# Four DMA copies of the mixing matrices instead of TensorE copies, and a burst of small products spread over four blocks

## The chip, the core and the metric

The kernel runs on one core of a Trainium2 chip. The metric is the device time of one execution in microseconds (us). The engines that matter here are TensorE (PE in the profile, its weight loads PEld), VectorE (DVE), ScalarE (ACT), GpSimd (POOL) and SyncE (SP). SP, ACT and POOL also issue DMAs; the name of such an issue in the profile is SPq, ACTq or POOLq.

## The reference

The program is two residual layers over x of shape 32 x 32 x 512 (1024 rows of 512 numbers). The first one begins with a small mixing of the 32 channels of each sample, by one of 16 matrices, chosen by a number that comes with the sample:

```python
def _L0_cond_ref(x, weights, condition):      # weights 16 x 32 x 32
    W = weights[condition]
    return jnp.einsum('bct,bcd->bdt', x, W)

x = x + _L0_ffn_ref(_L0_cond_ref(x, L0_cond_weights, itok_B_0_15), ...)
x = x + _L1_ffn_ref(_L1_cond_ref(x, itok_B_8_3872, ...), ...)
```

`_L0_ffn_ref` routes each row to 2 of 16 experts (softmax, best groups, best 2) and adds a shared expert. `_L1_cond_ref` convolves each of the 32 channels along time with a kernel that is computed from a few parameters, for channel h and time l:

```python
Cs = Cc * (jnp.exp(dtA) - 1.0) / A
K = 2.0 * jnp.einsum('hn,hnl->hl', Cs, jnp.exp(P)).real
```

`_L1_ffn_ref` is a dense layer with a latent branch and a layer norm.

## The kernel before

The program is written engine by engine, and the order of the instructions on each engine is the order in which they stand in the code. Engines wait for each other on semaphores (`wait_ge`), whose names are used below.

**The front** works on 8 tiles of 128 rows, 4 samples of 32 channels each. For each tile a block-diagonal matrix `wbd` of 128 x 128 is filled with the four chosen 32 x 32 matrices, so that one TensorE product mixes the tile. The 16 matrices come by one DMA of ACT's queue into `wraw`, on 32 partitions. A block of the diagonal on partitions 32b to 32b+31 has to be copied from the same partitions, so the matrices are needed four times, one below the other. Before, TensorE makes these copies: 8 products with a 32 x 32 identity fill banks 6 and 7 with four copies each (`wall_done`). DVE copies the blocks of seven tiles out of bank 6, ACT those of tile 2 out of bank 7, each block by an instruction whose place comes from a register. The registers are loaded from `condr` beforehand (`picked_matrices`).

TensorE then mixes tile i (`mixr_done`), ACT copies the result to `xstage` (`x_row`) and sends it to DRAM (`xrow`), TensorE transposes it, ACT writes the high part `ah`, and DVE the low part `al`. Every second tile TensorE adds the router's products (`router_logits`), which need `ah` and `al` of two more tiles. ACT waits once, between its first two tiles, for the router's loads (`router_in`), which stand behind `wraw` in its DMA queue. Beside this, DVE makes the low part `swl` of the shared expert's weights (`split_lo`), and after the front it runs the long chain of small steps of the routing. TensorE meanwhile has the shared expert's products (`shared_products`). Inside of one of them, `middle_product`, stand the two products over the chosen experts (`rank_products`), which wait for the routing (`msk_ok`).

**The blocks.** The rows go in 31 blocks of 128 through the experts. Each step n of the loop on TensorE has 8 products of 128 x 128 for block n (`L1606`), the output product of block n-2 (`L1574`) and the 4 transposes of block n+2 (`L1568`). POOL gathers the rows of each block by indirect DMA and scatters the results, and SP loads the experts' weights. An instruction on 32-bit numbers stands in the order once, and has two records in the trace, so that the 8 products are 16 records.

**The time kernel** of the convolution is made in parts along the blocks by DVE, ACT and POOL. Its last part is 32 small products on TensorE (128 x 16 weights, 64 columns), which stand all in step n = 15 behind that step's transposes. ACT copies the result at n = 16 (`kout`), DVE adds to it at n = 17, SP stores it at n = 18, and reads it back spread out for the convolution at n = 23 to 25.

## Time and profile before

| | |
|---|---|
| times of three runs | 343.67 (median), 340.64 and 344.4 us |
| the profiled execution: its own time | 343.47 us |
| its span, first to last instruction | 341.6 us |
| TensorE busy in the span | 324.8 us |
| mean granted clock of TensorE | 0.990 |

The profile is of one execution, and its own time stands 0.2 us from the median of the three runs. The span leaves out 1.9 us of that time. The rows further down are of this execution. Busy times of TensorE are modelled from the starts of its instructions, so that in the timeline the last instruction of a group overlaps the next group; the chain of waits counts each stretch of time once.

### The profile page before, as it was taken

The page shows a single profiled execution, that of the slowest core. Times are in us where ns is not written, and L with a number is a line of the kernel's source. Part 1 is how long each engine was busy: PE and PEld are TensorE (multiplying, and loading weights), DVE is VectorE, ACT ScalarE, POOL GpSimd, SP SyncE. Part 2 cuts the span into 40 slices and gives each one's busy share as a digit, 9 for nine tenths or more (in the row PEclk, how much of TensorE's full clock was granted, in tenths as well). Part 3 has the DMA queues.
Part 4 walks back from the last instruction along what each step waited for, and adds up shares of the span by engine and source line. Part 5 has one row for each costly group of instructions (what it writes and reads, how often), then busy time and mean ns, then how long its engine had stood idle before and what let it go on. Part 6 is the DMA issues. An engine that isn't in the chain of part 4 may idle for free.

```text
span 341.6 us, 5497 instructions
## 1 busy us (share of the span) xinstructions
PE 324.8 (95%) x1945; PEld 245.8 (72%) x1945; DVE 187.4 (55%) x375; ACT 115.3 (34%) x199; POOL 109.8 (32%) x131
## 2 busy tenths in 40 slices
PE   8998899999999599999998899899999999999994
PEld 2566788988887288888686444468888787888872
DVE  3747896888365122365469469537322446442366
ACT  1571312323722123363006833832231424222120
POOL 8243004356577546663400000699200000000000
PEclk9999999999999879999999999999999999999999
DMA  6999920796686629999969986000000000100002
GB/s 194 327 405 405 384 70 13 221 316 205 188 269 219 199 69 328 317 318 378 406 236 412 388 279 216 2 1 0 2 0 0 3 0 31 63 31 0 2 21 101
DMA packets 32830, 59.93 MB, mean 175 GB/s; under 512 B 7213, under 2 KB 8081, under 8 KB 32804
## 3 DMA queue, kind: packets, MB, share of 16 engines
q1 hardware_dynamic: 25764, 48.95, 41.6%
q0 software_dynamic: 4992, 8.42, 7.2%
q10 hardware_dynamic: 2048, 2.21, 1.8%
q8 instruction: 16, 0.26, 0.3%
q14 instruction: 10, 0.08, 0.1%
HBM read 55.02 MB, written 12.40 MB: 197 GB/s over the span
## 4 chain that ended last, share of the span: by engine, by line
PE 80%; DVE 10%; issue 5%; POOL 2%; ACT 2%; DMA 1%; ACTq 0%; DVEq 0%; POOLq 0%
PE bank L1606 15%; PE bank L435 13%; PE bank L437 12%; PE bank L436 12%; PE bank L1574 7%; PE bank L1679 5%; PE bank L1568 4%; PE bank L1434 2%; DVE acc L1259 2%; PE bank L1688 1%; PE bank L1384 1%; PE bank L1466 1%; PE bank L1390 1%; PE bank L1509 1%; DVE osum L1307 1%
## 5 line engine op out<-in xcount | busy, mean ns | idle before, releaser
L1606 PE MATMUL bank<-xt,ew 128*128 128x128 f32 x496 | 62.4, 280 | 0.0
L1606 PEld LDWEIGHTS bank<-xt,ew 128*128 128x128 f32 x496 | 59.6, 196 | 0.8 <-issue 0.7
L639 POOL DMA_INDIRECT xg<-xrow,tokx x31 | 33.3, 1073 | 38.9 <-DVE tokx L1077 25.2
L646 POOL DMA_INDIRECT ytok<-yout,dstx x31 | 31.9, 1029 | 33.3 <-DVE yout L1189 20.3
L1348 DVE TENSOR_TENSOR sq<-rel 128x512 f32<-128x512 f32 x16 | 13.3, 834 | 37.0 <-ACT rel L888 37.0
L1574 PE MATMUL bank<-ew,bhid 128*128 128x512 f32 x62 | 31.7, 595 | 0.0
L792 ACT ACTIVATE xt<-bank 128x512 f32<-128x512 f32 x31 | 18.4, 598 | 31.9 <-PE bank L1568 24.6
L1568 PEld LDWEIGHTS bank<-ident,xg 128*128 128x128 f32 x124 | 15.1, 141 | 16.1 <-issue 14.0
L435 PE MATMUL bank<-ah,uph 128*128 128x512 f32 x64 | 25.2, 394 | 0.9 <-issue 0.9
L435 PE MATMUL bank<-dnh,sqh 128*128 128x512 f32 x64 | 25.2, 393 | 0.4
L436 PE MATMUL bank<-dnl,sqh 128*128 128x512 f32 x64 | 24.9, 390 | 0.0
L437 PE MATMUL bank<-dnh,sql 128*128 128x512 f32 x64 | 24.9, 390 | 0.0
L437 PE MATMUL bank<-ah,upl 128*128 128x512 f32 x64 | 24.9, 389 | 0.0
L436 PE MATMUL bank<-al,uph 128*128 128x512 f32 x64 | 24.9, 389 | 0.0
L686 POOL TENSOR_TENSOR dnl<-dnraw,dnh 128x512 fp32r<-128x512 f32 x8 | 10.5, 1359 | 44.4 <-ACT dnh L855 44.4
L1189 DVE COPY yout<-bank 128x512 f32<-128x512 f32 x31 | 21.4, 689 | 2.6 <-PE bank L1574 0.6
L888 ACT ACTIVATE rel<-bank 128x512 f32<-128x512 f32 x16 | 9.6, 599 | 38.5 <-PE bank L437 38.4
L1200 DVE SCALAR_TENSOR_TENSOR bhid<-bank,b12d,bsil 128x128 f32<-128x128 f32 x15 | 5.3, 351 | 27.4 <-issue 21.3
L1568 PE MATMUL bank<-ident,xg 128*128 128x128 f32 x124 | 18.6, 274 | 0.9 <-issue 0.6
L1679 PE MATMUL bank<-toep,u_t 128*32 128x512 f32 (+3 forms) x256 | 18.7, 435 | 0.7 <-ACT u_t L831 0.7
L1351 DVE TENSOR_TENSOR sql<-sq,sqh 128x512 fp32r<-128x512 f32 x16 | 12.0, 751 | 11.2 <-PE bank L437 6.3
L1200 DVE SCALAR_TENSOR_TENSOR bhid<-bank,b,bsil 128x128 f32<-128x128 f32 x16 | 5.6, 348 | 20.2 <-ACT bsil L804 14.9
(316 smaller groups left out, 619.5 us busy)
## 6 DMA issues: line engine op xcount, KB each, us to landing
ew<-in_L_ffn_ew SPq DMA_DIRECT2D x51, 256.0 KB
ew<-in_L_ffn_ew SPq DMA_DIRECT2D x21, 512.0 KB, 11.9
toep<-kpad SPq DMA_DIRECT2D x4, 1536.0 KB, 17.6
acc<-in_x SPq DMA_DIRECT2D x4, 512.0 KB, 7.2
xrow<-xstage ACTq DMA_DIRECT2D x4, 512.0 KB, 7.7
yg_lo<-ytok SPq DMA_DIRECT2D x4, 512.0 KB, 4.9
yg_hi<-ytok SPq DMA_DIRECT2D x4, 512.0 KB, 8.1
upraw<-in_L_ffn_up_w SPq DMA_DIRECT2D x1, 2048.0 KB, 14.3
```

Of the source, the lines that this page charges most:

```text
L435: pe.matmul(dst, lh, rh, start=(start and k == 0), stop=False)
L436: pe.matmul(dst, lh, rl, start=False, stop=False)
L437: mm = pe.matmul(dst, ll, rh, start=False, stop=(stop and k == n_k - 1))
L639: pool.indirect_dma_start(xg[:, n % XGS, :], None, xrow, bass.IndirectOffsetOnAxis(ap=tokx[:, n:n + 1].bitcast(U32), axis=0), bounds_check ...
L646: pool.indirect_dma_start(ytok, bass.IndirectOffsetOnAxis(ap=dstx[:, n:n + 1].bitcast(U32), axis=0), yout[:, n % YOS, :], None, bounds_che ...
L792: act.activation(xt[:, n % 2, :, :], bank[n % 2][:, :].rearrange("p (k n) -> p k n", k=KC), ACT.Copy)\
L1189: dve.tensor_copy(yout[:, n % YOS, :], bank[6 + n % 2][:, :]).then_inc(yout_ok, 1)
L1348: tt(sq[:, v % 2, :], rel[:, v % 2, :], rel[:, v % 2, :], ALU.mult).then_inc(sq_ok, 1)
L1568: mm = pe.transpose(bank[n % 2][:, k * P:(k + 1) * P], xg[:, n % XGS, k * P:(k + 1) * P], ident[:, :])
L1574: pe.matmul(bank[6 + n % 2][:, :], bhid[:, n % BHS, :], ew[:, ring(n), W3], start=True, stop=True)\
L1606: mm = pe.matmul(bank[2 + n % 2][:, w * P:(w + 1) * P], ew[:, ring(n), col + k * P:col + (k + 1) * P], xt[:, n % 2, k, :], start=(k == 0), ...
L1679: mm = pe.matmul(bank[g % 3][j * B:(j + 1) * B, 0:T - k * P], u_t[:, h0 + j, k, :], toep[:, (h0 + j) % TS, k * P:T], start=(k == 0), stop= ...
```

## The change

The mixing matrices are loaded four times by DMA, each copy onto its own 32 partitions, and in another place in memory. The TensorE copies and their semaphore are gone; DVE and ACT copy the blocks out of `wraw`. SP no longer waits for the TensorE copies ahead of its weight loads. On DVE the comparison `before` moves ahead of the wait for the matrices, and `split_lo(0)` moves from tile 5 to tile 4. In `middle_product` one more group of three products stands ahead of `rank_products`. The 32 small products of the time kernel are spread over the steps n = 14 to 17, eight in each, and the three steps that follow (ACT, DVE, SP) are each two blocks later.

```diff
-        act.dma_start(wraw[:, :, :], cond_w.rearrange("k c d -> c k d")).then_inc(wraw_in, 16)
+        for b in range(BT):
+            act.dma_start(wraw[b * C:(b + 1) * C, :, :], cond_w.rearrange("k c d -> c k d")).then_inc(wraw_in, 16)
...
-        act.wait_ge(wall_done, 2)
+        act.wait_ge(wraw_in, 16 * BT)
         act.wait_ge(wbd_ok, 1)
...
-        dve.wait_ge(wall_done, 1)
-        for i, conds in dve_conds:
-            for b in range(BT):
-                dve.tensor_copy(diagonal(i, b), matrix(6, b, conds[b])).then_inc(wbd_ok, 1)
         dve.wait_ge(const_ok, PLACES)
         link(tt(before[:, :, :], prow[:, 0:E].unsqueeze(1).broadcast_to([P, E, E]),
                 prow[:, 0:E].unsqueeze(2).broadcast_to([P, E, E]), ALU.is_lt))
+        dve.wait_ge(wraw_in, 16 * BT)
+        for i, conds in dve_conds:
+            for b in range(BT):
+                dve.tensor_copy(diagonal(i, b), matrix(b, conds[b])).then_inc(wbd_ok, 1)
...
+            if i == 4:
+                split_lo(0)
             if i == 5:
-                split_lo(0)
...
-        pe.wait_ge(wraw_in, 16)
-        for w in (6, 7):
-            for b in range(BT):
-                mm = pe.matmul(bank[w][b * C:(b + 1) * C, :], ident[0:C, 0:C],
-                               wraw[:, :, :].rearrange("c k d -> c (k d)"), start=True, stop=True)
-            mm.then_inc(wall_done, 1)
...
-            split3(pe, bank[CBANK[1]][:, :], weights, tokens, 1, stop=False)
+            split3(pe, bank[CBANK[1]][:, :], weights, tokens, 2, stop=False)
             rank_products()
...
-            if n == 15:
-                pe.wait_ge(bd_ok, 1)
-                pe.wait_ge(lhs_ok, 2)
-                for m in range(HT // KQ):
-                    for lhs, rhs in ((lre_k, rre_k), (lim_k, rim_k)):
+            if KSTEP <= n < KSTEP + HT // KQ:
+                if n == KSTEP:
+                    pe.wait_ge(bd_ok, 1)
+                    pe.wait_ge(lhs_ok, 2)
+                m = n - KSTEP
+                for lhs, rhs in ((lre_k, rre_k), (lim_k, rim_k)):
```

**ACT at the start of the program**, before: one load of the matrices (`wraw`), then the router's three loads.

```order
L701 DMA wraw<-in_L_cond_weights 32x16x32
L702 DMA rwraw<-in_L_ffn_router_w 128x64
L703 DMA rb<-in_L_ffn_router_b 128x16
L704 DMA rb<-in_L_ffn_router_bias 128x16
L723 ACT_TABLE_LOAD
L723 ACTIVATE std<-warm 128x1
L442 TENSOR_LOAD condr
```

And with the change, where `wbd` is now filled out of `wraw`:

```order
L701 DMA wraw<-in_L_cond_weights 32x16x32 x4
L702 DMA rwraw<-in_L_ffn_router_w 128x64
L703 DMA rb<-in_L_ffn_router_b 128x16
L704 DMA rb<-in_L_ffn_router_bias 128x16
L723 ACT_TABLE_LOAD
L723 ACTIVATE std<-warm 128x1
L442 TENSOR_LOAD condr
```

Three DMAs of the matrices have come ahead of the router's loads, and the block copies wait for all four.

**TensorE at step 15 of the block loop**, before. `rre_k`, `rim_k`, `lre_k` and `lim_k` are the operands of the time kernel's products, `xt` and `ew` those of the block's.

```order
L1574 MATMUL bank<-ew,bhid 128x512
L1568 MATMUL bank<-ident,xg 128x128 x4
L1630 MATMUL bank<-rre_k,lre_k 16x64 x4
L1630 MATMUL bank<-rim_k,lim_k 16x64 x4
L1630 MATMUL bank<-rre_k,lre_k 16x64 x4
L1630 MATMUL bank<-rim_k,lim_k 16x64 x4
L1630 MATMUL bank<-rre_k,lre_k 16x64 x4
L1630 MATMUL bank<-rim_k,lim_k 16x64 x4
L1630 MATMUL bank<-rre_k,lre_k 16x64 x4
L1630 MATMUL bank<-rim_k,lim_k 16x64 x4
L1606 MATMUL bank<-xt,ew 128x128 x8
```

With the change, from the transposes of step 14 on (line numbers are 5 lower):

```order
L1563 MATMUL bank<-ident,xg 128x128 x4
L1625 MATMUL bank<-rre_k,lre_k 16x64 x4
L1625 MATMUL bank<-rim_k,lim_k 16x64 x4
L1601 MATMUL bank<-xt,ew 128x128 x8
L1569 MATMUL bank<-ew,bhid 128x512
L1563 MATMUL bank<-ident,xg 128x128 x4
L1625 MATMUL bank<-rre_k,lre_k 16x64 x4
L1625 MATMUL bank<-rim_k,lim_k 16x64 x4
L1601 MATMUL bank<-xt,ew 128x128 x8
L1569 MATMUL bank<-ew,bhid 128x512
L1563 MATMUL bank<-ident,xg 128x128 x4
```

The row of 32 small products is cut into four rows of 8, with 13 instructions of a block between two of them.

**DVE in the front**, before, from its comparison to the end of the low parts. `al` are the low parts of the 8 tiles, `swl` those of the shared expert's weights.

```order
L933 TENSOR_TENSOR before<-prow 128x256
L936 TENSOR_TENSOR rwc<-rwraw,rwc 128x4x16
L944 TENSOR_TENSOR al<-bank,ah 128x4x128 x6
L940 TENSOR_TENSOR swl<-swraw,swh 128x1024
L949 CAST dimh<-sw 128x16
L950 RECIPROCAL sw<-sw 128x16
L944 TENSOR_TENSOR al<-bank,ah 128x4x128 x2
L940 TENSOR_TENSOR swl<-swraw,swh 128x1024
```

With the change (the comparison stands ahead of the block copies now):

```order
L936 TENSOR_TENSOR rwc<-rwraw,rwc 128x4x16
L944 TENSOR_TENSOR al<-bank,ah 128x4x128 x5
L940 TENSOR_TENSOR swl<-swraw,swh 128x1024
L944 TENSOR_TENSOR al<-bank,ah 128x4x128
L950 CAST dimh<-sw 128x16
L951 RECIPROCAL sw<-sw 128x16
L944 TENSOR_TENSOR al<-bank,ah 128x4x128 x2
L940 TENSOR_TENSOR swl<-swraw,swh 128x1024
```

The first `swl` has moved one `al` up, and `dimh` with the reciprocal stays behind the sixth `al`.

## Rows read from the trace of the kernel before

**Rows 1.** Waits of PE, whole run (waiting line, releaser: total us, times, longest).
```profile
PE bank L1630 <- issue: 3.7, 5, 1.1
...
PE bank L1475 <- DVE w2t L991: 0.9, 1, 0.9
...
PE bank L1416 <- DVE al L944: 0.8, 1, 0.8
```

**Rows 2.** Timeline of PE, 0 to 30 us (start, us, engine, line, tiles, shape, records).
```profile
1.51 3.78 PE L1384 MATMUL bank<-warm 128*128 128x512 f32 x4 [1.51 <-DVE warm L920]
5.23 3.64 PE L1390 MATMUL bank<-wraw,ident 32*32 32x512 f32 x16
8.79 3.78 PE L1434 MATMUL bank<-acc,wbd 128*128 128x512 f32 x4
...
14.93 1.02 PE L1434 MATMUL bank<-acc,wbd 128*128 128x512 f32 x2
```

**Rows 3.** Timeline of ACT, 0 to 42 us; ACTq is its issue of a DMA.
```profile
0.80 0.40 ACTq L701 DMA_DIRECT2D wraw<-in_L_cond_weights  x1
...
2.24 0.45 ACTq L704 DMA_DIRECT2D rb<-in_L_ffn_router_bias  x1
...
11.40 0.25 ACT L734 ACTIVATE rwc<-rwraw 128x64 fp32r<-128x64 f32 x1
```

**Rows 4.** DVE: loads of condition numbers (view of tile condr), and its timeline.
```profile
L442 DVEq TENSOR_LOAD <-condr x7: 336/343/593, 3.2 to 5.6; - x7
...
7.34 6.08 DVE L931 COPY wbd<-bank 32x32 f32 x28 [4.22 <-PE bank L1390]
```

**Rows 5.** DMA issues at 0 to 1.3 and 2.4 to 3 us: KB, us to landing.
```profile
acc<-in_x SPq DMA_DIRECT2D x1, 512.0 KB, 4.0
wraw<-in_L_cond_weights ACTq DMA_DIRECT2D x1, 64.0 KB, 1.9
...
rb<-in_L_ffn_router_bias ACTq DMA_DIRECT2D x1, 8.0 KB, 7.5
```

**Rows 6.** DMA queues, 0 to 12 us: packets, MB, share (q1 SP's, q10 ACT's).
```profile
q1 hardware_dynamic: 1557, 2.76, 72.8%
q10 hardware_dynamic: 960, 0.11, 6.2%
```

**Rows 7.** DMA queues, 20.5 to 22.5 us.
```profile
q10 hardware_dynamic: 206, 0.42, 53.6%
q1 hardware_dynamic: 207, 0.40, 51.5%
```

**Rows 8.** Chain that ended last, 0 to 80 us (start us, us, what).
```profile
40.18 0.23 PE bank L435
```

**Rows 9.** Chain that ended last, 108 to 130 us.
```profile
113.13 0.33 PE bank L1630 x10
...
114.93 0.50 issue
...
118.27 1.49 PE bank L1630 x46
119.76 3.67 PE bank L1606 x16
...
124.73 1.79 PE bank L1606 x16
```

**Rows 10.** Windows at 108 to 128 us: length, busy by engine, granted clock, DMA share, GB/s.
```profile
113.00:116.00 3.00, 1.17 (x16) 0.44 (x14) 0.00 (x0) 0.19 (x1) 2.12 (x3) 1.00 0.90 251
116.00:117.00 1.00, 0.15 (x4) 0.23 (x4) 0.00 (x0) 0.00 (x0) 0.96 (x1) 0.71 0.88 326
...
119.00:123.00 4.00, 4.00 (x44) 3.80 (x34) 0.69 (x2) 0.20 (x1) 2.04 (x2) 0.50 0.03 4
```

**Rows 11.** Timelines of SP and of ACT, 96 to 122 us.
```profile
112.55 1.42 SPq L527 DMA_DIRECT2D ew<-in_L_ffn_ew  x2
...
118.34 0.37 ACT L804 ACTIVATE bsil<-bank,b 128x128 f32<-128x128 f32 x1 [5.15 <-remote]
```

33 lines of the change are left out of this document (16 added, 17 removed).

## The prediction

> **What bounds the kernel now.** TensorE is busy for 324.8 of the 341.6 us, so I read its waits first. Over the whole run the longest in sum is at line 1630, the 32 small products of the time kernel: 3.7 us in five pieces, put down to "issue", which means that no semaphore in the trace explains them. Behind it come 0.9 us for the routing at line 1475 and 0.8 us for the low parts at line 1416 [rows 1]. Next I read the chain of waits at these places. The chain is TensorE's own for nearly all of the run, so a microsecond that TensorE loses or gains in the front or in the block loop is one of the total.
>
> In the front the timeline of TensorE shows two warm-up products to 5.29 us, the copies of the matrices to 8.87, and the first mixing product at 8.79 [rows 2]. The copies are the gate: DVE starts its 28 block copies at 7.34, after 4.2 us of waiting for them [rows 4], while the first load of x, issued before 1.3 us, took 4.0 us and so was in by 5.3 us [rows 5]. In the block loop the chain has the small products from 113.1 to 119.8 us, then a block's 16 records that take 3.67 us where the same 16 take 1.79 us a block later [rows 9].
>
> **The small products.** Their work is short: 46 of the 64 records take 1.49 us [rows 9], 32 ns each, so all 64 take 2.1 us. They have 119.76 - 113.13 = 6.63 us, so 4.5 us are stall. And the stall has a sequel. TensorE had 1.17 us of busy time between 113 and 116 us; the granted clock was 0.71 in the next microsecond, and 0.50 from 119 to 123 [rows 10]. That is the lower of the two levels, 1.2 GHz, and the following block pays 3.67 - 1.79 = 1.9 us for it [rows 9]. The places together lose 4.5 + 1.9 = 6.4 us. The page "TensorE: Matmul & The Clock Gate" of the Trainium skill (Part 1) says that an idle spell brings the clock to half rate until sustained work releases it; the trace agrees, with 0.50.
>
> With the change eight products follow the transposes of each of steps 14 to 17. Their work stays on the path, a fourth of 2.1 us each time, since TensorE has no idle time there to hide it. What of the stall stays depends on its cause, which the trace does not tell. For the burst as the cause speaks that the program has only one such burst (128 product and load records in a row) and only one such stall, and that the last 46 records then run freely. Against it speaks that others stall too: SP needs 1.42 us for two issues at 112.55, and ACT starts a step at 118.34 after 5.15 us of waiting for something that the profile calls "remote" [rows 11]. I take it that the burst is the cause and that cutting it frees the 6.4 us. The other end is 0. The steps moved behind it (ACT, DVE, SP, two blocks later each) cost nothing: their instructions are the same, and the store of the result at step 20 has three blocks before it is read back at step 23. If that cover failed, the read-back would be late, and its first user is the convolution, behind all blocks.
>
> **The matrices by DMA.** Removed are TensorE's copies, 3.64 us. TensorE would still have to wait for DVE's first four block copies, a seventh of 6.08 us, 0.87 us [rows 4]. So the first mixing product comes 0.87 us after the last copy of the matrices has landed, or after DVE is free, whichever is later. DVE's seven loads of condition numbers start until 5.6 us and take 0.34 each [rows 4], and the comparison stands behind them now: it is free at about 6.4 us. If the DMAs were in by then, mixing would begin at 7.3 instead of 8.8, a gain of 1.5 us.
>
> Are they? One copy alone took 1.9 us from its issue at 0.80 [rows 3, 5]. The next three are issued every 0.42 us, the last at 2.1. But by then the loads of x are on the same DMA engines, issued from before 1.3 us on. Three things bear on the last copy's landing.
> - If ACT's queue were on its own, it would land at 2.1 + 1.9 = 4.0 us. This is the lower end.
> - The nearest row in place and queue is the load of the router's bias: issued by ACT at 2.24 us, 8 KB, landed after 7.5 us, at 9.7 [rows 3, 5]. A copy of the matrices issued at 2.1 has eight times its bytes, in rows of 128 bytes.
> - The queues share in turns. Where both had work, ACT's moved 206 packets in two microseconds and SP's 207 [rows 7]. One matrix copy is 32 x 16 = 512 packets (rows of 128 bytes), so three are 1536. Before, SP's queue needed the whole of 0 to 12 us for its 1557 packets [rows 6]. With one packet of ACT for one of SP, the last copy lands at about 12 us or shortly after, say 13.5 with its own packets' time and the landing on top. This is the upper end, somewhat stretched.
>
> I take 12.0, nearest to the count of packets, since both queues have work from 2 us on. Mixing then begins at 12.0 + 0.87 = 12.9 instead of 8.8: a loss of 4.1 us (range: gain of 1.5 to loss of 5.6). Nothing hides it, because everything up to the routing hangs on the mixing. That TensorE now idles from 5.3 us on costs nothing further by these rows: the first mixing passes run slowly as it is, 3.78 us for four records against 1.02 for two later on [rows 2].
>
> A rule of the skill speaks against this part. "DMA: Bandwidth & Descriptors", section Issuing engines are not separate DMA queues, says that DMAs from all engines run on the same 16 DMA engines and interleave, whoever issued them. The trace agrees by its 206 to 207. By the rule the sum is the one that follows; without it, with a landing at 4.0 us, it would be 5.6 us lower.
>
> Behind the copies in ACT's queue stand the router's three loads. ACT needed them at 11.40 us before, without waiting [rows 3], 4.1 us after the block copies began. With the new order they are the last in the queue, and might come somewhat more than 4.1 us after the matrices. I count 0.4 us (0 to 1.5). SP's dropped wait gives nothing: at that place in its queue the copies had long been made.
>
> **The two orders.** `split_lo(0)` one tile earlier uses idle time of DVE ahead of the sixth tile. It can give at most the 0.8 us that TensorE waits at line 1416 [rows 1]; ACT's `ah` of the last tile is late next, so I count 0.4. In `middle_product` three products of 0.23 us [rows 8], 0.7 us, move ahead of the wait of 0.9 us for the routing [rows 1]. They fit into it whole, 0.2 us of wait remain, and the routing gets its products no later: 0.7 us.
>
> **Sum.** 343.47 - 6.4 (small products) + 4.1 (matrices late) + 0.4 (router's loads) - 0.4 - 0.7 = 340.5 us. The profiled execution stands 0.2 us below the median of the three runs, so this is also about 0.9% below the median.
>
> **Rivals.**
> - **The stall is not the burst's.** ACT and SP were slow in the same stretch [rows 11], so a congestion of the DMAs or of memory may hold everyone until about 118 us, whatever TensorE has to do. The split then gives nothing, and the late matrices decide: 340.5 + 6.4 = 346.9 us, slower than before. It is slower from the point where less than 3.4 us of the 6.4 come back. Chance 0.28.
> - **The stall is partly left.** Eight products at a time still stutter, but TensorE does not idle long enough to lose its clock, or the reverse: about half, 3.2 us, comes back. 343.7 us, no change. Chance 0.20.
> - **The matrices are early.** The copies interleave better than one for one, or the descriptors reach the engines ahead of those of x; mixing begins at 7.3 us. Against it stands the router's bias with its 7.5 us. With the stall gone: 340.5 - 4.1 - 1.5 - 0.4 = 334.5 us. Chance 0.14; with a landing between, at 8 us, it would be 336.5.
> - **The forecast**, stall gone and matrices late, has 0.38.
>
> **How the numbers follow.** One per cent, 3.4 us, is about what this measurement can tell from no change. Within the forecast the landing's bounds alone give 337 to 342, within the second rival 344 to 348.4. The range 335.5 to 348.5 leaves out the ends of the early and of the late case. Faster by over 1% (below 340.2) are most of the early case, 0.12, and a good half of the forecast, 0.21, where the landing is before 11.7 us: 0.33. Slower by over 1% (above 347.1) are near half of the first rival and a bit of surprise: 0.19. The rest, 0.48, is within 1%.
>
> **What would show it.** In the changed profile: the landing of the four `wraw` loads, and the first mixing product 0.9 us after the last (I expect 12.9; 7.3 if the early rival holds). The four groups of small products should take 0.5 us each, with no wait "issue" and a granted clock of 1.00 between 100 and 125 us; under the first rival the same gaps appear at other instructions of TensorE. The wait at line 1475's successor should be about 0.2 us. The prediction is wrong if the front's end moves by less than 1 us, or if a stall of some microseconds stands in the block loop at all.

## The result, and where the time went

The changed kernel takes 349.4 us in the median of four runs (349.0 to 350.5), against 342.7 us for the kernel before beside it (four runs, 340.6 to 344.4): a ratio of 1.021, with a 95% interval of 1.016 to 1.026. The forecast was 340.5. In this and in every ratio below, a run more than 1.5% above the fastest of its kernel is left out. The profiled execution after has 349.01 us, a span of 347.2 us against 341.6.

**First view: the whole run.** The page's row of busy time, and part 4, the chain that ended last, of the changed kernel:

```profile
PE 320.9 (92%) x1929; PEld 243.1 (70%) x1929; DVE 187.1 (54%) x375; ACT 114.7 (33%) x199; POOL 110.9 (32%) x131
...
PE 63%; DVE 11%; DMA 9%; issue 8%; POOL 3%; SPq 1%; ACT 1%; another core or an unknown queue 1%; ACTq 1%; DVEq 0%; POOLq 0%
```

TensorE works 3.9 us less (324.8 before) in a span 5.6 us longer. The chain has 63% of the span on TensorE, where it had 80% before, and 9% on DMAs, where it had 1%.

**Second view: by stage.** The block loop has one group of 16 product records a block, so the start of the first one marks where a kernel stands. The small products of step n stand ahead of block n+1. These columns are worked out from such groups of each profile: start of block 0, then the length from block 0 to 13, 13 to 17, 17 to 24, 24 to 30, and from there to the end of the span. All kernels of the study but e4 stand here, since the experiments are read from it too.

```
kernel                  block 0   0-13   13-17   17-24   24-30  30-end   span
before                    62.85  39.41   22.30   21.59   18.93  176.52  341.6
after                     65.09  39.41   20.11   22.64   22.68  177.27  347.2
e1_orders                 61.62  39.41   22.62   21.59   18.93  176.54  340.7
e2_four_loads             66.50  39.41   22.21   21.59   18.93  177.26  345.9
e3_four_parts             59.86  39.41   22.88   22.23   21.94  178.07  344.4
e5_late_sw3               64.91  39.41   22.82   22.23   18.93  177.00  345.3
e6_sbuf_copies            66.31  39.41   20.07   21.59   18.93  176.60  342.9
e7_no_products            60.07  39.41   22.53   21.59   18.93  176.58  339.1
e8_no_chain               62.81  39.41   22.33   21.59   18.93  176.53  341.6
e9_chain_on_dve           62.58  39.41   19.26   21.59   18.93  178.04  339.8
e10_warm_after            63.30  39.41   21.66   22.23   22.64  177.56  346.8
e11_loads_early           59.70  39.41   21.75   21.59   18.93  177.12  338.5
e12_orders_chain_dve      58.83  39.41   18.90   21.59   18.93  176.54  334.2
e13_short_gathers         59.66  39.41   23.06   21.59   18.93  176.55  339.2
e14_gathers_held          62.51  39.41   17.33   27.68   19.83  178.65  345.4
e15_matrices_first        59.52  39.41   23.01   22.23   22.33  177.51  344.0
e16_best_first            61.27  39.84   16.62   21.59   18.93  176.45  334.7
e17_best_capped           62.01  39.41   16.39   23.12   21.60  177.87  340.4
e18_change_mended         59.39  39.41   17.40   22.23   21.00  177.27  336.7
```

From before to after: front +2.24, blocks 13 to 17 -2.19, 17 to 24 +1.05, 24 to 30 +3.75, the rest +0.75, together 5.6 us. The front and the stretch of the stall, on which the prediction spent its words, cancel. What made the kernel slower lies between blocks 17 and 30, mostly in the last six.

**The front.** Answering to [rows 2] and [rows 4], the timelines of TensorE and of DVE in the changed kernel (start, length, line, what, and in brackets the wait before it), and the DMAs of the matrices:

```profile
1.51 3.78 PE L1385 MATMUL bank<-warm 128*128 128x512 f32 x4 [1.51 <-DVE warm L920]
11.80 3.75 PE L1429 MATMUL bank<-acc,wbd 128*128 128x512 f32 x4 [6.50 <-DVE wbd L934]
```

```profile
6.04 0.42 DVE L929 TENSOR_TENSOR before<-prow 128x256 f32<-128x256 f32 x1 [2.93 <-issue]
10.91 6.49 DVE L934 COPY wbd<-wraw 32x32 f32 x28 [4.45 <-DMA wraw<-in_L_cond_weights]
```

```profile
L701 ACTq DMA_DIRECT2D wraw<-in_L_cond_weights x4: 399/508/512, 0.8 to 2.3; - x4
...
DMA to landing us min/median/max: 1.9/5.4/8.4
```

The fourth copy is issued at 2.30 us and takes 8.4: it lands at 10.7, DVE starts at 10.9, the mixing at 11.8, 3.0 us later than before and 1.1 after the landing. By block 0 the delay is down to 2.2 us, so 0.8 came back, which fits the two orders.

**The stall.** The chain of waits of the changed kernel from block 15 on, and three windows (the last columns are the granted clock, the share of the DMA engines and GB/s), to set beside [rows 9] and [rows 10]:

```profile
112.43 0.35 PE bank L1625 x16
112.78 1.76 PE bank L1601 x14
114.54 0.39 issue
...
115.32 1.04 issue
...
117.04 0.74 issue
...
119.85 0.78 issue
```

```profile
113.00:116.00 3.00, 1.93 (x16) 1.64 (x15) 0.46 (x1) 0.60 (x1) 2.39 (x3) 1.00 0.76 253
116.00:119.00 3.00, 1.70 (x4) 0.65 (x4) 0.00 (x0) 0.00 (x0) 2.39 (x3) 1.00 0.87 248
119.00:123.00 4.00, 3.03 (x35) 2.67 (x36) 0.95 (x2) 0.85 (x2) 0.15 (x1) 1.00 0.40 118
```

A fourth of the small products takes 0.35 us. But the waits "issue" are still there, now mostly at the lines of the block's own products (1601, 1569, 1563): from 111 us on they add up to 4.0 us, against 4.3 before. Only the clock held: 1.00 where it had been 0.50 before.

**The last blocks.** ACT's timeline near its step 23, and from the chain of waits the pieces that lead to it:

```profile
150.64 0.60 ACT L792 ACTIVATE xt<-bank 128x512 f32<-128x512 f32 x1 [2.52 <-PE bank L1563]
154.00 1.06 ACT L823 ACTIVATE sw3h<-sw3raw 128x1024 fp32r<-128x1024 f32 x1 [2.76 <-DMA kpad<-kout]
154.97 0.35 ACT L804 ACTIVATE bsil<-bank,b12d 128x128 f32<-128x128 f32 x1
```

```profile
148.30 5.68 DMA kpad<-kout
...
158.62 7.26 DMA xg<-xrow,tokx
```

ACT stands 2.8 us at its step 23, waiting for the store of the time kernel's rows, which SP now issues from 146.8 us on and which lands at 154.0, 7.2 us later. Behind ACT stand the blocks, and when they go on, a gather needs 7.3 us. Before, the same store was issued at 139.7, and no engine waited for it:

```profile
139.67 2.01 SPq L539 DMA_DIRECT2D kpad<-kout  x4
146.85 1.05 ACT L823 ACTIVATE sw3h<-sw3raw 128x1024 fp32r<-128x1024 f32 x1
```

ACT came to its step 23 there 7.2 us after the store's first issue, so there was hardly any time to spare: in three kernels that store at step 18, as before (e4, e6 and e7), ACT waited 0.5 to 1.0 us for it.

### The profile page after: what moved, and what is told of

Same layout as the page of the kernel before. It is cut to its first block, busy times and chain, and to the rows that moved or that the text cites. A ratio compares the mean times of both kernels' runs of the same rounds, so it can differ in the third digit from the quotient of the medians.

```text
span 347.2 us, 5467 instructions
## 1 busy us (share of the span) xinstructions
PE 320.9 (92%) x1929; PEld 243.1 (70%) x1929; DVE 187.1 (54%) x375; ACT 114.7 (33%) x199; POOL 110.9 (32%) x131
## 4 chain that ended last, share of the span: by engine, by line
PE 63%; DVE 11%; DMA 9%; issue 8%; POOL 3%; SPq 1%; ACT 1%; another core or an unknown queue 1%; ACTq 1%; DVEq 0%; POOLq 0%
PE bank L435 12%; PE bank L436 11%; PE bank L437 11%; PE bank L1601 9%; PE bank L1569 4%; DMA xg<-xrow,tokx 3%; PE bank L1429 3%; PE bank L1563 3%; PE bank L1674 3%; DMA wraw<-in_L_cond_weights 2%; DVE acc L1260 2%; DMA kpad<-kout 2%; DVE upl L1280 1%; DMA ytok<-yout,dstx 1%
## 5 line engine op out<-in xcount | busy, mean ns | idle before, releaser
L1601 PE MATMUL bank<-xt,ew 128*128 128x128 f32 x496 | 61.3, 276 | 2.8 <-issue 1.6
L1601 PEld LDWEIGHTS bank<-xt,ew 128*128 128x128 f32 x496 | 58.1, 192 | 4.3 <-issue 2.3
L685 POOL TENSOR_TENSOR dnl<-dnraw,dnh 128x512 fp32r<-128x512 f32 x8 | 10.5, 1349 | 45.3 <-ACT dnh L855 45.3
L1429 PE MATMUL bank<-acc,wbd 128*128 128x512 f32 x16 | 10.6, 765 | 6.5 <-DVE wbd L934 6.5
## 6 DMA issues: line engine op xcount, KB each, us to landing
ew<-in_L_ffn_ew SPq DMA_DIRECT2D x21, 512.0 KB, 11.9
toep<-kpad SPq DMA_DIRECT2D x4, 1536.0 KB, 17.6
```

The source lines that it names most:

```text
L1429: pe.matmul(bank[2 * (i % 3) + 1][:, :], wbd[:, i, :], acc[:, i, :], start=True, stop=True)\
L1601: mm = pe.matmul(bank[2 + n % 2][:, w * P:(w + 1) * P], ew[:, ring(n), col + k * P:col + (k + 1) * P], xt[:, n % 2, k, :], start=(k == 0), ...
```

## The experiments

Ratios are to the kernel before, run on the same chip beside each, with 95% intervals. A stage's length is from the table above.

### The parts of the change, each alone

e1_orders is the two changes of order:

```diff
-            if i == 5:
-                split_lo(0)
+            if i == 4:
+                split_lo(0)
...
-            split3(pe, bank[CBANK[1]][:, :], weights, tokens, 1, stop=False)
+            split3(pe, bank[CBANK[1]][:, :], weights, tokens, 2, stop=False)
```

> The kernel before with the two changes of order alone (the split of the low parts one tile earlier, two products ahead of the routing in place of one). Theory, from the changed kernel's trace: its first block of experts starts 2.24 us later while its first mixing product starts 3.0 us later, so the orders give 0.75 us; the first block should start at 62.1 instead of 62.85 and the time be 0.8 us below the kernel before. Rival: the wait for the routing grows by what is taken away, because the routing itself is late: no change, 62.8.

Measured: 340.4 us, ratio 0.998 (0.994 to 1.003), and in the profile block 0 starts 1.23 us earlier. The waits are 0.5 at line 1417 (0.8 before) and 0.2 for the routing (0.9 before):

```profile
PE bank L1417 <- DVE al L944: 0.5, 1, 0.5
PE bank L1476 <- DVE w2t L992: 0.2, 1, 0.2
```

That is near the prediction's 0.4 + 0.7. A gain of this size is below what the timing tells.

e2_four_loads is the matrices by DMA alone (the diff of the change without its other parts).

> The kernel before with the matrices loaded in four copies by DMA, nothing else. Theory: only the start of the mixing moves, 3.0 us later (11.8 instead of 8.8), and all behind it, so the time is 3 us above the kernel before and the block loop's own intervals stay as they were. Rival: the loads of x take the place of the copies and the later mixing finds its tiles ready, so that half of it comes back by the first block: +1.5 us.

Measured: 1.016 (1.009 to 1.023). The first mixing product starts at 12.58, block 0 at 66.50, 3.65 us later, and the block loop is untouched up to block 30. Next to nothing of the delay (3.79 us at the mixing) comes back, and the part behind the blocks is 0.74 us longer.

e3_four_parts is the products in four parts and the three later steps alone.

> The kernel before with the small products in four parts and the three steps behind them two blocks later, nothing else. Theory A: ACT waits at step 23 for the stored kernel rows, which are stored two blocks later and land only after that step; in the changed kernel this cost 3.7 us from block 24 to block 29, and the parts themselves gained 1.1 us up to block 18. So +2.6 us, with ACT's wait for the store in the trace and blocks 25 to 29 late. Theory B: the late loss of the changed kernel came from its front being shifted against the transfers, not from the store: -1 to -2 us, and blocks 24 to 30 every 3.1 us.

Measured: 1.017 (1.010 to 1.024), or 5.8 us (5.0 between the medians), twice what theory A gave. The late loss is there, 3.0 us from block 24 to 30, with ACT waiting 5.1 us for the store; 1.6 us more are lost behind the blocks, which was not explained. But blocks 13 to 17 take 22.88 us against 22.30: alone, the split doesn't shorten the stall at all. And this profile showed something in the front, which it has in common with the kernel before:

```profile
5.22 1.99 PE L1390 MATMUL bank<-wraw,ident 32*32 32x512 f32 x16
7.44 2.00 PE L1434 MATMUL bank<-acc,wbd 128*128 128x512 f32 x4 [0.23 <-DVE wbd L931]
9.28 0.64 PE L1398 MATMUL bank<-ident,xstage 128*128 128x128 f32 x4
```

The same copies took 3.64 us and the same four mixing records 3.78 in the profile before [rows 2]. The clock came up some microseconds earlier in this execution, and block 0 starts at 59.86 instead of 62.85. The view of windows doesn't show this, since it prints 1.00 where the trace has no record of the clock: the trace's first record, at the level 1.00, stands at 5.4 us here and at 14.0 in the profile before. Of the twelve profiles of kernels in which TensorE makes the copies, five have it at 4.9 to 6.0 us and seven at 13.3 to 14.1. The times of the kernel before fall in two groups as well: of thirteen in one call, six took 339.6 to 341.5 us and seven 343.0 to 344.0. That these are the same two kinds is likely, and not shown run by run.

e4_two_parts cuts the products in two, at steps 14 and 15, and leaves the later steps where they were.

```diff
-            if n == 15:
+            if 14 <= n < 14 + HT // KQ // 2:
...
-                for m in range(HT // KQ):
+                for m in range((n - 14) * 2, (n - 14) * 2 + 2):
```

> The kernel before with the small products in two parts of 16 at steps 14 and 15, and the copy, the sum and the store where they were (steps 16, 17, 18). Theory A (the store's lateness is what costs): no late loss, and the gain of the parts alone, -1 to -2 us; the spell in which TensorE loses time without a semaphore stays, at other instructions, while GpSimd issues its gathers and scatters back to back. Rival, the burst of 64 short instructions is itself the cause: half of the stall, -3 us or better. Under a third, any split loses: +0.5 us or more.

Measured: 0.999 (0.995 to 1.003), no gain, by six of its eleven runs (340.7 to 342.4 us). The other five took 347.2 to 349.7 us, the profiled one among them, so its stages aren't in the table. What set them apart was not looked into.

### Is it the store that makes the last blocks late?

```diff
-            if n == 23:
+            if n == 26:
                 act.wait_ge(kpad_in, 16 * KQ)
...
-            elif n == 24:
+            elif n == 27:
                 dve.wait_ge(swh_ok, 3)
```

> The changed kernel whole, and ACT's step 23 (the wait for the stored kernel rows and the copy of a shared expert's weights into their place) made step 26, DVE's step 24 behind it made 27. Theory A: ACT's wait for the store is what made blocks 25 to 30 late; now the store has landed before ACT comes to it, blocks 24 to 30 start every 3.1 us, and the time is 3 to 4 us below the changed kernel, 1.0 to 1.2% above the kernel before. Rival: the delay in this stretch is in the transfers (the late loads of weights, the store, and the reads of the matrix rows one on the other, with gathers of 7 us), ACT only showed it: 0 to 1 us below the changed kernel, 2% above the kernel before.

Measured: 1.014 (1.009 to 1.019) against 1.021 for the change, and blocks 24 to 30 take 18.93 us, to the hundredth what they took before. ACT's timeline has the copy without a wait:

```profile
158.83 0.60 ACT L792 ACTIVATE xt<-bank 128x512 f32<-128x512 f32 x1 [0.93 <-PE bank L1563]
159.32 1.05 ACT L823 ACTIVATE sw3h<-sw3raw 128x1024 fp32r<-128x1024 f32 x1
```

So the 3.75 us of these blocks are the price of ACT's wait and of what followed from it. The timing gives 2.6 of them; blocks 13 to 17 take 22.82 us in this profile, so the change's 20.11 did not come back.

### What is the stall?

e7_no_products:

```diff
-                for m in range(HT // KQ):
+                for m in range(1):
```

> The kernel before with 28 of the 32 small product pairs' halves left out: of the four parts only the first m is computed, 8 products in place of 32, so that the time kernel is wrong in most of its rows; all waits and later steps are as before. Burst theory: with no burst there is no stall: the time is 6.4 + 1.6 (the work left out) = 8 us below the kernel before, and TensorE has no gap of its own between 105 and 120 us. Theory of GpSimd's catch-up (its gathers and scatters run back to back from 102.5 to 117 us, and all gaps of TensorE in six profiles lie in that stretch): the gaps stay and move to the blocks' own instructions, and only 1.6 to 3.5 us come back.

Measured: 0.999 (0.993 to 1.005). TensorE's timeline with a quarter of the products:

```profile
110.11 0.30 PE L1630 MATMUL bank<-rre_k,lre_k 128*16 128x64 f32 x8
111.38 0.27 PE L1630 MATMUL bank<-rim_k,lim_k 128*16 128x64 f32 x2 [0.97 <-issue]
112.85 0.22 PE L1630 MATMUL bank<-rim_k,lim_k 128*16 128x64 f32 x1 [1.19 <-issue]
...
115.69 0.37 PE L1630 MATMUL bank<-rim_k,lim_k 128*16 128x64 f32 x2 [1.13 <-issue]
115.99 3.78 PE L1606 MATMUL bank<-xt,ew 128*128 128x128 f32 x16
```

Sixteen records take 5.9 us, and the block behind them 3.78, twice its length. Three quarters of the work gone, and blocks 13 to 17 take 22.53 us (22.30 before). The burst is not the cause: TensorE is drawn out there with a fourth of the work as well.

e8_no_chain and e9_chain_on_dve ask whether it is GpSimd being late. GpSimd runs 15 small operations of the time kernel between two gathers, and has to catch up afterwards. The diff is that of e9; e8 has two copies on GpSimd in the place of the 15 operations.

```diff
-        move(0, 15)
-        pool.wait_ge(s4v_ok, POWERS)
-        link(pool.tensor_scalar(w[NR], er, -1.0, None, ALU.add))
...
-        pool.tensor_tensor(w[CIN], w[X1], w[X2], ALU.subtract).then_inc(s4p_ok, 1)
-        move(15, NB + AHEAD)
+        move(0, NB + AHEAD)
...
+        def s4_coef():
+            link(dve.tensor_scalar(w[NR], er, -1.0, None, ALU.add))
...
+            elif n == 11:
+                s4_coef()
```

> The kernel before without GpSimd's chain of 15 small operations between its gathers (two copies stand in their place, so the coefficients of the time kernel are wrong); everything else is as before. Theory of the catch-up: without the 5 us of the chain GpSimd isn't late, its gathers and scatters don't run back to back afterwards, and TensorE has no gaps and no lower clock between 105 and 125 us: 5 to 8 us below the kernel before. Burst theory: the stall stays at the small products, and at most 0.6 us comes back.

> The kernel before with the same chain of 15 operations run by DVE at its step 11, which is empty, in place of GpSimd; the same numbers are computed. Theory of the catch-up: as without the chain, less what DVE's chain costs if it holds a block (15 operations and their waits, 2 to 3 us against some 1.5 us of free time a block): 4 to 7 us below the kernel before. Burst theory: no change, or up to 1.5 us slower for the held block.

Measured: without the chain 1.002 (0.996 to 1.007), and the stall as before, 22.33 us. With the chain on DVE 0.990 (0.982 to 0.998), and the stretch 3.0 us shorter (3.4 in e12, which has the same edit), while the part behind the blocks is 1.5 us longer. The four runs are 335.6, 339.9, 340.0 and 341.6 us, and the ratio leaves out the last, which is the profiled one; with it the medians give 0.995. So the shorter stretch is the firm result here, and the gain in time rests on e12. The two contradict the plain catch-up theory: taking the chain out altogether should help at least as much. The profile of e8 shows GpSimd issuing back to back all the same, from 93.2 to 107.4 (with one rest of 1.0 us) and from 110.6 to 118.3 us.

e11_loads_early takes the weights' loads out of the stretch:

```diff
-        return d * 7 // 5 if d < RING else LATE_STEPS[d - RING]
+        return d if d < RING else LATE_STEPS[d - RING]
```

> The kernel before with the loads of the later experts' weights issued as soon as a place is free (one at each of the steps 0 to 13) in place of seven in five steps each; the last three stay at steps 20 to 22. So between 105 and 120 us only gathers and scatters use the DMA engines. Theory (the weights' loads together with the gathers hold up the engines' instructions there): no gaps of TensorE between 105 and 120 us, 5 to 7 us below the kernel before. Rival (the loads have no part in it): the gaps stay, ending 16 us after the start of block 13, and the time is the same within 1 us.

Measured: 0.994 (0.988 to 1.000), blocks 13 to 17 21.75 us. The ratio leaves out three of the eight runs (342.7 to 343.6 us), which look like the later kind of e3's two; against the kernel before's earlier kind (340.6 in the mean) four of the other five are level, at 340.3 to 340.8. The gaps stay, so the loads have little part in it.

By now fourteen profiles showed one thing in common. GpSimd issues its gathers and scatters back to back, one each 1.33 us, and TensorE's last gap ends 0.9 to 1.5 us after the end of that stretch in all but one (e11, 2.8). In the profile before this is the last issue of the stretch, and the last gap ends at 118.27 [rows 9]:

```profile
115.94 1.03 POOL L639 DMA_INDIRECT xg<-xrow,tokx x1 [0.31 <-issue]
```

Two experiments ask which of the two follows the other:

```diff
+            rows = 16 if 15 <= n <= 20 else P
...
-            pool.indirect_dma_start(xg[:, n % XGS, :], None, xrow,
+            pool.indirect_dma_start(xg[0:rows, n % XGS, :], None, xrow,
```

```diff
             wait(pool, bx_done, n - XGS + 1)
+            if 17 <= n <= 20:
+                pool.wait_ge(bh_done, n - 2)
```

> The kernel before with the gathers 15 to 20, which GpSimd issues back to back from 102.5 to 117 us, fetching 16 rows each in place of 128, so that six blocks work on rows of earlier ones and the result is wrong there. Theory C1 (the packets of the gathers, with the weights' loads, congest the stretch and hold up all engines): no gaps of TensorE between 105 and 120 us, or less than half, 3 us or more below the kernel before. Theory C2 (it is GpSimd's issuing itself, whatever it moves): if a short gather takes GpSimd as long, the gaps stay and end 1.0 to 1.5 us after GpSimd's last issue; no change. Theory C3 (neither): the gaps stay and their end no longer follows GpSimd's.

> The kernel before with one more wait on GpSimd: gathers 17 to 20 each wait for the products of the block three before theirs, so that GpSimd can't run ahead while TensorE stands. In 13 of 14 profiles TensorE's last gap ended 0.9 to 1.5 us after GpSimd's back-to-back stretch. If GpSimd's stretch is what holds the others (C1 or C2), it is now cut at about 113 us, and TensorE's last gap ends at 113 to 115 instead of 118.3, with blocks 16 to 19 late by their gathers (3 to 4 us from issue to landing against 3 us of lead), 0 to 3 us below the kernel before. If the order is the other way (GpSimd stops because TensorE stood and no more rows are due), the gaps still end at about 118 us and the kernel is 1 to 4 us slower.

Measured: with short gathers 1.003 (0.998 to 1.007), and 23.06 us from block 13 to 17. A gather of 16 rows occupies GpSimd for 0.92 to 0.94 us (the first 1.00), one of 128 rows for 1.03 (the first 1.10), so its stretch is nearly as long as before, and so is the stall: the gathers' packets don't matter. The scatters and the loads of weights were left as they were.

```profile
112.67 0.92 POOL L640 DMA_INDIRECT xg<-xrow,tokx x1 [0.30 <-issue]
```

With the gathers held 1.011 (1.004 to 1.017; two timed runs) in all, but the stretch falls to 17.33 us. GpSimd's timeline in that kernel:

```profile
109.25 1.03 POOL L641 DMA_INDIRECT xg<-xrow,tokx x1 [1.54 <-PE bank L1608]
110.59 1.01 POOL L648 DMA_INDIRECT ytok<-yout,dstx x1 [0.30 <-issue]
112.92 1.02 POOL L641 DMA_INDIRECT xg<-xrow,tokx x1 [1.32 <-PE bank L1608]
114.25 1.01 POOL L648 DMA_INDIRECT ytok<-yout,dstx x1 [0.30 <-issue]
118.94 1.03 POOL L641 DMA_INDIRECT xg<-xrow,tokx x1 [3.67 <-PE bank L1608]
```

It rests where it ran on before. TensorE passes 40 of the 64 small records within 0.8 us from 113.2 us on, has gaps of 0.41 and 0.45 us during and right behind the scatter of 114.25, and is through at 116.1. What this kernel loses in all, it loses behind the stretch: 27.68 us from block 17 to 24, with late gathers, and 2.1 us behind the blocks.

### The landing of the matrices, and TensorE's clock

e6_sbuf_copies loads the matrices once, as before, and makes the other three copies from that one inside the local memory, 96 packets of 2048 bytes in place of 1536 of 128:

```diff
+        act.wait_ge(wraw_in, 16)
+        for b in range(1, BT):
+            act.dma_start(wraw[b * C:(b + 1) * C, :, :], wraw[0:C, :, :]).then_inc(wraw_in, 16)
```

> The kernel before with one load of the matrices from memory, as before, and the three other copies made from it by DMA within the local memory, in rows of 2048 bytes (96 packets in place of 1536), issued by ACT behind the router's loads; TensorE makes no copies. Theory (the late landing is a matter of the packets that stand in turn with those of x): the copies are issued at about 5 us and land at 7 to 8.5, the first mixing product starts at 8 to 9.5, about where it was before: the time is 0 to 1 us from the kernel before, 3 to 4 below the four loads. Rival (anything behind the loads of x waits for them, whatever its count): landing at 10 or later, and 2 us or more above the kernel before.

Measured: 1.015 (1.009 to 1.021). ACT's timeline:

```profile
2.85 2.35 ACTq L705 DMA_DIRECT2D wraw<-wraw  x3
12.04 0.98 ACT L731 ACTIVATE wbd<-wraw 32x32 f32 x4 [5.31 <-DMA wraw<-wraw]
```

A sixteenth of the packets, with the same bytes, are in at 11.9 us, later than the 10.7 of the change. The three copies were issued from 2.85 us on, their first packet moved at 8.5, and they landed at 10.4, 11.0 and 11.9, while the last load of x, issued at 2.69, landed at 12.6. So it isn't packets in turn with those of x. In the change the same is seen: the second, third and fourth load of the matrices landed at 5.8, 8.0 and 10.7 us, and the loads of x issued just ahead of them at 5.5, 7.3 and (the third and the fourth) 9.0 and 10.5. A copy issued behind the loads of x comes in with them, whatever the number of its packets.

e10_warm_after is the change with WARM = 5 in place of 2.

> The changed kernel whole, with five warm-up products on TensorE in place of two, which fill its idle time from 5.3 us on; the matrices arrive as late as before. Theory: the idle time has a price of its own, since TensorE meets the mixing at the lower clock; with the filling the first four mixing records take 2.0 us, as in the one profile where the clock was up early, and not 3.75, and the first block starts 1.7 to 2 us earlier (63.2 instead of 65.1). The prediction's step, by which the idling costs nothing further, says: no change.

Measured, by the profile (two timed runs, 1.016): block 0 at 63.30 instead of 65.09, though its matrices were 0.6 us later.

```profile
1.52 7.51 PE L1385 MATMUL bank<-warm 128*128 128x512 f32 x10 [1.52 <-DVE warm L920]
12.40 1.95 PE L1429 MATMUL bank<-acc,wbd 128*128 128x512 f32 x4 [3.37 <-issue]
```

1.95 us instead of 3.75 for the same four records, half: the two levels of the clock. This is one profile, and by e3 the moment changes from one execution to the next, so I set all of them side by side. The trace's first record of the clock at 1.00 stands at 16.7 to 17.6 us in the four kernels in which TensorE makes no copies and has two warm-up products (the change, e2, e5, e6), and at 5.7 to 7.7 in the four with three or five of them (e10, e15, e16, e18). With TensorE's copies it came early in five of twelve. So the copies that the change removed seem to have been the second half of TensorE's warm-up.

e15_matrices_first is the change with SP issuing two of the four loads ahead of those of x, and WARM = 3:

```diff
+        for b in range(2):
+            sp.dma_start(wraw[b * C:(b + 1) * C, :, :], cond_w.rearrange("k c d -> c k d")).then_inc(wraw_in, 16)
         for j in range(4):
             sp.dma_start(acc[:, 2 * j:2 * j + 2, :],
```

> The changed kernel whole with two of the four loads of the matrices issued by SP ahead of the loads of x, the other two by ACT as its first two, and three warm-up products in place of two. Theory (a load issued behind those of x lands when x has landed, whatever its size, since SBUF copies of 96 packets landed at 12 as well): now all four are ahead, land at 3.5 to 5 us, DVE is free at 6.4, and the first mixing product starts at 7.3 to 7.6 us, at the higher clock (four records in 2.0 us); the first block starts at 58.5 to 60 instead of 65.1, and the time is 5 to 6 us below the changed kernel. Rival (the loads of x are held up by as much as the matrices gain): the first mixing product waits for x until 9 us or later.

Measured, by the profile (two timed runs, 1.013):

```profile
1.51 5.49 PE L1387 MATMUL bank<-warm 128*128 128x512 f32 x6 [1.51 <-DVE warm L922]
8.37 1.10 PE L1431 MATMUL bank<-acc,wbd 128*128 128x512 f32 x2 [1.37 <-DVE wbd L936]
```

```profile
5.22 0.98 ACT L732 ACTIVATE wbd<-wraw 32x32 f32 x4 [0.45 <-DMA wraw<-in_L_cond_weights]
```

The matrices are in at 5.1 us, the mixing starts at 8.4 and block 0 at 59.5, 5.6 us earlier than in the change. It is where the kernel before is when its clock comes up early (59.7 to 60.1), so the DMAs buy at best what TensorE's copies gave; e15 has the two orders besides, and the kernel with TensorE's copies, the orders and an early clock (e12) is at 58.8. The time, 346.7 us, is only 2.7 below the change where 5 to 6 were expected: blocks 13 to 17 take 23.01 us here, 2.9 more than in the change's profile.

### Putting parts together

e12_orders_chain_dve is the two orders and the chain on DVE, without splitting and without the DMA copies.

> The kernel before with the two changes of order and the chain of 15 small operations on DVE in place of GpSimd, the two parts that did not lose by themselves (0.998 and 0.990 of the kernel before). If their gains add: 1.0 to 1.5% below the kernel before, about 337.5. If the stall swallows the earlier arrival: no better than the chain alone, 1.0% below.

Measured: 336.0 us (four runs, 335.7 to 336.3), 0.979 (0.974 to 0.985): the best of the study. A part of it is the clock: its profile has the early one, and its runs lie within 0.6 us, so probably all had it, where about half of the kernel before's do. Against the early runs of the kernel before in that call (mean of six 340.6) it is 4.6 us, 1.3%: 1.2 from the orders, 3.4 from the stretch of blocks 13 to 17.

e16_best_first adds the matrices by DMA, two loads ahead of x, WARM = 3.

> The two orders, the chain of 15 operations on DVE, and the matrices by DMA with two loads ahead of x and three warm-up products; the small products in one burst and the three steps behind them where they were. Theory: the front ends where it ends with TensorE's copies when the clock is up early (58.8 us), so this is 0.979 of the kernel before, as with the copies; if the early matrices gain another 0.1 to 1 us, 0.977. Rival: the earlier x traffic is pushed back and the front ends 1 us or more later: 0.982.

Measured: 337.6 us, 0.988 (0.984 to 0.992). Block 0 is at 61.27, 2.4 us behind e12: the first mixing products start at 8.4, but the clock fell between them (four records of the mixing in 1.10 and 1.59 us). The DMA copies don't pay here either.

e17_best_capped is e12 with a softer hold (gathers 18 to 21 wait for the block four before).

> The two orders and the chain on DVE (0.979 of the kernel before), and gathers 18 to 21 each wait for the products of the block four before theirs; in the profile of that kernel gathers 18 and 19 would not be delayed by it, and gather 20, issued at 109.7 while TensorE stood, would wait for block 16. Theory (GpSimd's issuing is what holds the engines): its stretch ends at 109.4 instead of 110.75, TensorE's last gap ends about 110.5 instead of 111.7, and the lower clock behind it may go too: 1 to 2.4 us below 336.0, 0.973 to 0.976 of the kernel before. Rival (the earlier result of the held gathers came from something else, or the held gathers now land late): no change or up to 1 us slower, 0.979 to 0.982.

Measured: 1.000 (0.996 to 1.003) by twelve runs, the gain of e12 gone, and yet blocks 13 to 17 in 16.39 us, 2.5 less than in e12. The granted clock stays at 1.00 there, where e12 has 0.50 from 111.8 to 115.2 us.

```profile
111.54 1.02 POOL L641 DMA_INDIRECT xg<-xrow,tokx x1 [1.26 <-PE bank L1575]
112.87 1.02 POOL L648 DMA_INDIRECT ytok<-yout,dstx x1 [0.30 <-issue]
117.51 1.02 POOL L641 DMA_INDIRECT xg<-xrow,tokx x1 [3.61 <-PE bank L1613]
```

Blocks 17 to 30 take 44.72 us, 4.2 more than in e12, since GpSimd now issues back to back from 120.6 to 156.8 with two rests of 3.2 and 3.4 us. What it didn't catch up while TensorE stood, it owes later. Part of the loss against e12 is the clock, late here (block 0 at 62.0).

e18_change_mended is the change with e5, e15 and the chain on DVE.

> The changed kernel with its products in four parts and the steps behind them two blocks later, and with the losses found mended: ACT's wait for the store at step 26, two of the matrices' loads ahead of x with three warm-up products, and the chain of 15 operations on DVE. If the accounts are right, the front ends at 59 to 61 us (60.4 in the mean of the two kernels with matrices first), the last blocks lose nothing, and the stall costs 3 us less than before: 337 to 340 us, 0.985 to 0.993 of the kernel before. If splitting in itself costs more (the parts alone left blocks 13 to 18 1.1 us longer than before), it is at the upper end, and above the unsplit version with matrices first (0.988).

Measured: 338.9 us, 0.993 (0.989 to 0.996). The accounts close for the front (59.4) and the stall (17.40). The last blocks still lose 2.1 us (21.00), with a wait of 1.1 us for a gather, which looks like the debt of GpSimd once more. Split and mended, the products are 1.2 us behind the unsplit e16, though the two were timed in different calls (by their ratios, 0.993 and 0.988, it is 0.5%).

## Why the prediction was wrong

The sum was 343.47 - 6.4 + 4.1 + 0.4 - 0.4 - 0.7 = 340.5. The same terms as measured in the profile after: -1.1 for the small products (-2.2 up to block 17, +1.1 behind), +3.0 for the matrices, 0 for the router, -0.8 for the two orders together, and two terms that the sum didn't have, +3.75 for ACT's wait and +0.75 behind the blocks: 343.5 + 5.6 = 349.1.

- **"I take it that the burst is the cause and that cutting it frees the 6.4 us": wrong**, and the largest error: 1.1 us came back. The first rival had it right that the stall is not the burst's. Its sign was in [rows 11]: SP and ACT were as slow as TensorE in that stretch, which a burst on TensorE doesn't explain. e7 refutes the burst, e3 shows that the split alone doesn't shorten the stretch. What the change did gain there, it gained at the clock (1.00 instead of 0.50). The split doesn't secure it: e3, e5, e10 and e15 have the same spread and fell to 0.50 in that stretch, which took them 21.7 to 23.0 us, and e6 has the burst whole and took 20.07.
- **The work of the small products, 2.1 us, was taken at the lower clock.** The 46 records of 1.49 us ran at a granted clock of 0.50 [rows 9, 10]. In the change a fourth takes 0.35 us at 1.00, so all 64 are 1.4 us, and the stall was 5.2 us and not 4.5.
- **The steps moved behind it, which I put at nothing: wrong.** I looked for the reader of the stored rows and named the convolution. ACT waits for the same semaphore at step 23, since the copy that it makes there goes into the region of the time kernel's tables, and the store's landing is the event that the code waits for before it reuses that region. The store was issued 7.1 us later than before, and landed 7.2 us after its first issue. The cover was not three blocks: before, ACT came to its step just 7.2 us after that issue, and with the store two steps later it had to wait. That cost 3.75 us (e5). An engine that waits before it reuses memory is a reader of the semaphore too.
- **The landing at 12.0 us, the mixing at 12.9: nearly right in size** (10.7 and 11.8, a loss of 3.0 instead of 4.1), but by the wrong mechanism. The count of packets in turn would have put e6's 96 packets at 7 to 8.5; the last of them landed at 11.9. The order of issue against the loads of x decides (e15: 5.1). The profile before could have shown it: the router's bias, issued at 2.24 us, landed at 9.75, and the load of x issued just ahead of it, at 2.18, landed at 9.80. The rule of the Trainium skill that I weighed ("DMA: Bandwidth & Descriptors", Issuing engines are not separate DMA queues) stands: ACT's queue was no way around SP's loads.
- **"That TensorE now idles from 5.3 us on costs nothing further": wrong.** In the profile before, the first mixing was at the lower clock as it was. But that was one kind of run of two. e10 puts 1.8 us on it, and e3 shows 3.0 us in the kernel before itself. All four profiles with the idling have the clock late, so the better kind seems to be lost to it; four are few, and the runs with the loads alone (e2) still spread over 3 us. The page "TensorE: Matmul & The Clock Gate" of the Trainium skill (Part 1) says that sustained work releases the clock. The trace agrees in part, with 1.95 us behind 7.5 us of warm-up work and 3.75 us behind idling; but the kernel before had worked from 1.5 to 8.8 us without a pause, and its mixing took 3.78 us all the same.
- **The router's loads, +0.4: nothing.** ACT copied them at 14.50 without waiting.
- **The orders, -0.4 and -0.7: right** (e1: 1.23 in the profile; the waits fell to 0.5 and 0.2, in the change too, where 0.8 us came of it by block 0).
- **The rivals.** The first one came true in that the split gives nothing, but its 346.9 us lacked ACT's wait; its reason, a congestion of the DMAs or of memory, is not borne out, since neither earlier loads of weights (e11) nor short gathers (e13) ended the stall. The range ended at 348.5 because every bound was on the terms that I had seen; the bound of the one that I had put at nothing, with the words "if that cover failed", was never priced.

What stays open: by what path GpSimd's issuing of gathers and scatters stretches the instructions of TensorE, SP and ACT, if it is the issuing itself, and why this happens from about block 14 on and not at 85 to 90 us, where it also issues back to back (four in a row there, eleven here). e14 and e17 show that holding it shortens the stretch, e13 that the size of its gathers doesn't matter. The loading of instructions is not the cause as far as the trace shows: in the profile before their queues move nothing between 102 and 119 us. Why leaving the chain out (e8) doesn't help where moving it to DVE (e9, e12) does was not settled. Nor was it tried to leave scatters out. The 0.75 us behind the blocks was seen only as one more wait of TensorE for DVE's last sums; e2 has it without the split, and other kernels up to 2.1 us (e14).

## What to carry to other kernels

When a step moves later, list every wait on its semaphore, those that only free memory included, and price each as if its cover were gone. When several engines stand in the same microseconds, look for what they share before blaming the instruction that stands there, and ask whether the helper engine's backlog is being worked off meanwhile: a stall removed may be a debt that falls due later. Before taking work off an engine in the first microseconds, ask whether it is what brings that engine's clock up. Issue small urgent loads ahead of large ones.

## What the runs showed of the hardware that I had not expected

- Three DMAs of 32 packets each inside the local memory, issued from 2.85 us on by ACT, landed at 10.4, 11.0 and 11.9 us, behind 2 MB that SP had begun to load before them; ACT's load issued at 0.80 took 2.0 us (e6).
- The same first products run at either clock by the execution: 1.99 (e3) or 3.64 us (before) for the 16 copies that follow 3.78 us of warm-up, and block 0 starts 3.0 us apart.
- An indirect gather of 16 rows occupies GpSimd for 0.92 to 0.94 us (e13), one of 128 rows for 1.03 us (before).
- While GpSimd issued such transfers back to back, single instructions of TensorE came some 0.72 us apart (113.99, 114.71, 115.43 in the profile before), and SP needed 0.70 us for one DMA issue.
